# Grouped-query attention on one core: three reduced-precision value products instead of one full one, two units behind the scores, with normalisation on ScalarE and two steps on GpSimd

## Reference, cut to what matters

```python
nh, nkv, hd = 32, 8, 128
q = (x @ Wq).reshape(B, S, nh, hd).transpose(0, 2, 1, 3)
k = (x @ Wk).reshape(B, S, nkv, hd).transpose(0, 2, 1, 3)
v = (x @ Wv).reshape(B, S, nkv, hd).transpose(0, 2, 1, 3)
q = q * cos + rotate_half(q) * sin          # k likewise
logits = einsum('bhqd,bhkd->bhqk', q, repeat(k)) / sqrt(hd)   # causal mask
attn = softmax(logits)
out = einsum('bhqk,bhkd->bhqd', attn, repeat(v))
return out.transpose(0, 2, 1, 3).reshape(B, S, nh * hd) @ Wo
```

## Time and profile before

| | us |
|---|---|
| median of three runs | 2526.03 (2522.1 to 2527.65) |
| the profiled execution | 2533.18 |
| its span, first to last instruction | 2530.8 |
| the attention stage in it, from its first projection to its last merge | 1649.72 to about 2464 |
| one pass in it | 101.0 |

### The profile page before, as it was taken

One profiled execution on the slowest core, in us unless ns is written; L12 is line 12 of the kernel. 1 busy time (PEld: TensorE's weight loads), 2 busy tenths in 40 slices (PEclk: granted clock), 3 DMA queues, 4 the chain that ended last, 5 costly groups with the idle time before them and its releaser, 6 DMA issues. The chain is left out here.

```text
span 2530.8 us, 40532 instructions
## 1 busy us (share of the span) xinstructions
PE 2471.5 (98%) x12630; PEld 1861.0 (74%) x12630; DVE 1555.9 (61%) x2790; ACT 1392.1 (55%) x2155; POOL 1134.9 (45%) x1140
## 2 busy tenths in 40 slices
PE   8999999999999999999998999899999999999997
PEld 4677777777777777777775688778888888888874
DVE  6666666666666666666664522375756657557556
ACT  3677777777777777777776432232423424324231
POOL 1556555555555565556554243243434334334210
PEclk8999999999999999999999999999999999999998
DMA  6122222222222222222221422111001010010001
GB/s 213 42 45 55 45 53 47 51 53 44 53 46 57 46 53 44 53 46 54 45 53 38 139 88 88 65 44 42 17 25 41 0 41 17 25 41 17 1 3 52
DMA packets 47611, 125.38 MB, mean 50 GB/s; under 512 B 6034, under 2 KB 23442, under 8 KB 41427
## 3 DMA queue, kind: packets, MB, share of 16 engines
q1 hardware_dynamic: 47570, 124.85, 18.5%
HBM read 80.27 MB, written 10.49 MB: 36 GB/s over the span
## 5 line engine op out<-in xcount | busy, mean ns | idle before, releaser
L427 DVE TENSOR_REDUCE row_max<-ps_max 128x1 f32<-128x512 f32 x1024 | 670.4, 687 | 196.7 <-PE ps_max L517 174.9
L292 POOL TENSOR_TENSOR p_parts<-probs,p_parts 128x1024 f16<-128x1024 f32 x256 | 547.6, 2148 | 369.0 <-ACT p_parts L346 368.1
L341 ACT ACTIVATE probs<-ps_score 128x1024 f32<-128x1024 f32 x512 | 523.1, 1022 | 240.4 <-PE ps_score L533 218.6
L531 PE MATMUL ps_score<-Q,K 128*128 128x512 f32 x1024 | 408.1, 398 | 2.1 <-ACT probs L341 2.1
L533 PE MATMUL ps_score<-Q,K 97*128 97x512 f32 x1024 | 406.7, 397 | 0.0
L517 PE MATMUL ps_max<-KX,Q 68*128 68x512 f32 x1024 | 378.8, 411 | 2.2 <-DVE row_max L427 2.1
L421 DVE TENSOR_TENSOR Q<-ps_x,Q 64x512 fp32r<-64x512 f32 x254 | 175.1, 689 | 242.5 <-ACT Q L336 238.8
L346 ACT ACTIVATE p_parts<-probs 128x1024 f16<-128x1024 f32 x256 | 269.4, 1053 | 4.0
L517 PEld LDWEIGHTS ps_max<-KX,Q 68*128 68x128 f32 x1024 | 189.6, 190 | 75.0 <-issue 28.1
L531 PEld LDWEIGHTS ps_score<-Q,K 128*128 128x128 f32 x1024 | 194.2, 190 | 61.7 <-ACT probs L341 13.5
L533 PEld LDWEIGHTS ps_score<-Q,K 97*128 97x128 f32 x1024 | 195.0, 190 | 39.4
(11 more groups left out here) (269 smaller groups left out, 4387.6 us busy)
## 6 DMA issues: line engine op xcount, KB each, us to landing
Q<-Q SPq DMA_DIRECT2D x64, 512.0 KB, 4.3
ffn_raw<-in_w_ffn SPq DMA_DIRECT2D x22, 768.0 KB, 4.4
w_raw<-in_w_qrope SPq DMA_DIRECT2D x32, 512.0 KB, 3.6
wq_raw<-in_wq SPq DMA_DIRECT2D x8, 1024.0 KB, 5.5
wo_raw<-in_wo SPq DMA_DIRECT2D x8, 1024.0 KB, 4.8
content_k<-probs SPq DMA_DIRECT2D x8, 512.0 KB, 6.4
Q<-content_q SPq DMA_DIRECT2D x64, 64.0 KB
K<-content_k SPq DMA_DIRECT2D x64, 64.0 KB
```

The source lines that it names most:

```text
L292: pool.tensor_tensor(p_lo[:, j, :, :], probs[:, j, 0:PAIRED, :], p_hi[:, j, :, :], ALU.subtract)\
L341: act.activation(probs[:, j, 2 * half:2 * half + 2, :], ps_score[half][:, :, :], ACT.Exp, scale=SCALE).then_inc(exped, 1)
L427: dve.tensor_reduce(row_max[:, t, j:j + 1], ps_max[t % 2][:, :], axis=AXX, op=ALU.max)\
L531: pe.matmul(ps_score[half][:, k, :], K1[:, b, t * P:(t + 1) * P], Q1[:, b, j, :], start=True, stop=False)
```

## The change

1. The value product is made of three fp32r products per tile in place of one in float32. V and the turned probabilities therefore get a high and a low part: ACT writes the high ones, DVE the low ones (`low_values`, `low_turned`), out of the same PSUM bank.
2. On PE, `outputs(u-2)` and the third turn piece of u-2 stand in iteration u, the outputs behind the projection; turn pieces 0 and 1 of u-1 come last in the iteration. Turn piece k waits for the low part of the piece two before it (`t_low`), which frees its bank. The outputs of unit 6 stand behind the loop, and merges are ordered by head, so that those that need units 6 and 7 wait last (`o_low`). Turn piece 2 of unit 7 stands between two merges.
3. The four scalings of the probabilities are moved from DVE to ACT (L1493 becomes four activations with a scale); DVE keeps the reciprocal. `probs` is packed tightly.
4. The rope's sum is moved from DVE to POOL, in front of POOL's two steps.
5. ACT copies the output from PSUM to `o_raw`, and POOL makes its high and low part (`split_out`), in place of ACT and DVE.

```diff
--- before.py
+++ after.py
...
+        V = [buf(f"v_{k}", [P, NB, ST, P], F32R) for k in ("hi", "lo")]
+        by_sin = buf("by_sin", [P, 2, S])
         roped = buf("roped", [P, 2, S])
-        probs = buf("probs1", [P, 2, ST, S])
-        probsT = buf("probsT", [P, 3, S])
+        ROWS = [P * t * (t + 1) // 2 for t in range(ST + 1)]
+        probs = buf("probs1", [P, 2, ROWS[ST]])
+        TURNED = [(0, S), (S, S), (2 * S, 2 * P)]
+        probsT = [buf(f"probsT_{k}", [P, 2 * S + 2 * P], F32R) for k in ("hi", "lo")]
+        values_T = probs[:, 1, 0:NB * S].rearrange("p (b s) -> p b s", b=NB)
+        o_raw = buf("o_raw", [P, 2, S])
         O = [buf(f"o_{k}", [P, NB, GQ, S], F32R) for k in ("hi", "lo")]
         minus_max = buf("minus_max", [P, ST])
         sums = buf("sums", [P, 2, ST])
...
-
+            def rope(n, at, parts, take):
+
+                pool.wait_ge(taken, take + 1)
+                pool.sem_inc(gate_pool, 1)
+                pool.tensor_tensor(roped[:, at, :], roped[:, at, :], by_sin[:, at, :], ALU.add).then_inc(summed, 1)
                 pool.wait_ge(summed, n + 1)
                 pool.sem_inc(gate_pool, 1)
                 pool.tensor_copy(parts[0], roped[:, at, :]).then_inc(r_high, 1)
                 pool.wait_ge(r_high, n + 1)
+                pool.sem_inc(gate_pool, 1)
                 pool.tensor_tensor(parts[1], roped[:, at, :], parts[0], ALU.subtract).then_inc(r_low, 1)
 
...
+
+                pool.wait_ge(o_taken, ONE + i + 1)
+                pool.sem_inc(gate_pool, 1)
+                pool.tensor_copy(O[0][:, u % 2, u // 2, :], o_raw[:, u % 2, :]).then_inc(o_step, 1)
+                pool.wait_ge(o_step, i + 1)
+                pool.sem_inc(gate_pool, 1)
+                pool.tensor_tensor(O[1][:, u % 2, u // 2, :], o_raw[:, u % 2, :], O[0][:, u % 2, u // 2, :],
+                                   ALU.subtract).then_inc(o_low, 1)
+
+            pool.sem_inc(o_low, TWO)
             for b in range(NB):
...
-                    rope_query(r + u - 2, u, u % 2)
+                    rope_query(r + u - 2, u, u % 2, tk + take_query(u))
+                    if u >= 4:
+                        split_out(i + u - 4, u - 4)
                     if u == 2:
                         pool.wait_ge(wo_in, 16 * (kv + 1))
...
-                        rope_query(r + NU - 1 + 2 * b, b, 1)
+                        rope_key(r + NU - 2 + 2 * b, b, tk + take_next(2 * b))
+                        if b == 1:
+                            split_out(i + NU - 3, NU - 3)
+                            split_out(i + NU - 2, NU - 2)
+                        rope_query(r + NU - 1 + 2 * b, b, 1, tk + take_next(2 * b + 1))
                         if b == 0:
+                            split_out(i + NU - 4, NU - 4)
                             split_kv(1, s + n + 1)
+                    split_out(i + NU - 1, NU - 1)
                     for h in range(1, GQ):
                         split_q(h, s + n + 1 + h)
+                else:
+                    for u in range(NU - 4, NU):
...
+                act.wait_ge(inverted, i + 1)
+                for t in range(ST):
+                    row = probs[:, u % 2, ROWS[t]:ROWS[t + 1]]
+                    ins = act.activation(row, row, ACT.Copy, scale=inverse[:, t:t + 1])
+                ins.then_inc(normed, 1)
+
             def take_turned(kv, u, k):
...
 
             def take_outputs(kv, u):
 
                 i = NU * kv + u
                 act.wait_ge(pv_made, i + 1)
-                act.activation(O[0][:, u % 2, u // 2, :], ps_o[:, :], ACT.Copy).then_inc(o_high, 1)
+                act.wait_ge(o_low, i + 1)
+                act.activation(o_raw[:, u % 2, :], ps_o[:, :], ACT.Copy).then_inc(o_taken, 1)
 
...
-                softmax(i, 0)
+                ALL, BEGIN, REST = slice(0, ST), slice(0, 1), slice(1, ST)
+                softmax(i, 0, ALL)
+                normalise(i, 0)
                 values(kv, 0)
                 values(kv, 1)
                 turned_values(kv, 0)
                 turned_values(kv, 1)
                 for u in range(1, NU):
+                    if u >= 2:
+                        act.wait_ge(turned, 3 * (i + u - 1))
+                    softmax(i + u, u, BEGIN)
+                    if u >= 2:
+                        take_turned(kv, u - 2, 2)
+                    softmax(i + u, u, REST)
+                    if u >= 2:
+                        take_outputs(kv, u - 2)
                     take_turned(kv, u - 1, 0)
                     take_turned(kv, u - 1, 1)
-                    softmax(i + u, u)
-                    take_turned(kv, u - 1, 2)
-                    take_outputs(kv, u - 1)
+                    normalise(i + u, u)
+                take_turned(kv, NU - 2, 2)
+                take_outputs(kv, NU - 2)
                 for k in range(3):
                     take_turned(kv, NU - 1, k)
                 take_outputs(kv, NU - 1)
...
-                if not first:
-                    dve.wait_ge(summed, n)
                 if not first and not second:
...
-                dve.wait_ge(taken, take + 1)
-                dve.tensor_tensor(roped[:, at, :], roped[:, at, :], by_sin[:, :], ALU.add).then_inc(summed, 1)
 
...
+            def invert(i, u):
                 dve.wait_ge(exped, ONE + ST * (i + 1))
                 dve.reciprocal(inverse[:, :], sums[:, u % 2, :]).then_inc(inverted, 1)
-                dve.wait_ge(inverted, i + 1)
-                for t in range(ST):
-                    n = (t + 1) * P
-                    ins = dve.tensor_scalar(probs[:, u % 2, t, 0:n], probs[:, u % 2, t, 0:n], inverse[:, t:t + 1],
-                                            None, ALU.mult)
-                ins.then_inc(normed, 1)
-
-            def low_o(i, u):
-                dve.wait_ge(o_high, i + 1)
-                dve.tensor_tensor(O[1][:, u % 2, u // 2, :], ps_o[:, :], O[0][:, u % 2, u // 2, :], ALU.subtract)\
-                   .then_inc(o_low, 1)
-
-            dve.sem_inc(o_low, ONE)
+
+            def low_values(kv, b):
+                dve.wait_ge(v_high, NB * kv + b + 1)
+                dve.tensor_tensor(V[1][:, b, :, :], ps_t[b][:, :].rearrange("p (t n) -> p t n", t=ST), V[0][:, b, :, :],
+                                  ALU.subtract).then_inc(v_low, 1)
+
+            def low_turned(i, u, k):
+                dve.wait_ge(t_high, 3 * i + k + 1)
+                at, n = TURNED[k]
+                dve.tensor_tensor(probsT[1][:, at:at + n], ps_t[(u + k) % 2][:, 0:n], probsT[0][:, at:at + n],
+                                  ALU.subtract).then_inc(t_low, 1)
+
+            dve.sem_inc(t_low, TWO)
...
                 maxima(i)
-                normalise(i, 0)
+                invert(i, 0)
+                for b in range(NB):
+                    low_values(kv, b)
                 rope(r, ring + ring_query(2), (START + ring_query(2)) % 2, 0, tk, 0)
+
...
                     maxima(i + u)
-                    normalise(i + u, u)
+                    if u >= 2:
+                        low_turned(i + u - 2, u - 2, 2)
                     if u < NU - 2:
                         rope(r + u, ring + ring_query(u + 2), (START + ring_query(u + 2)) % 2, 0, tk + u, u % 2)
-                        low_o(i + u - 1, u - 1)
-                    else:
-                        for k in range(NU - u) if not last else ():
-                            at = 2 * (u % 2) + k
-                            rope(r + NU - 2 + at, ring + ring_next(at), (START + ring_next(at)) % 2, 1 - k, tk + take_next(at), k)
-                        low_o(i + u - 1, u - 1)
+                    elif not last:
+                        for at in (0, 1) if u == NU - 2 else (2,):
+                            rope_next(at)
+                    invert(i + u, u)
+                    low_turned(i + u - 1, u - 1, 0)
+                    low_turned(i + u - 1, u - 1, 1)
+                low_turned(i + NU - 2, NU - 2, 2)
                 if not last:
-                    rope(r + NU + 1, ring + ring_next(3), (START + ring_next(3)) % 2, 0, tk + take_next(3), 1)
+                    rope_next(3)
+                low_turned(i + NU - 1, NU - 1, 0)
+                low_turned(i + NU - 1, NU - 1, 1)
                 add_out(0)
-                add_out(1)
-                low_o(i + NU - 1, NU - 1)
-                for j in range(2, TT):
+                low_turned(i + NU - 1, NU - 1, 2)
+                for j in range(1, TT):
                     add_out(j)
 
...
                     pe.wait_ge(normed, i + 1)
-                if k == 2:
-                    pe.wait_ge(t_taken, 3 * i + 1)
+                pe.wait_ge(t_low, TWO + 3 * i + k - 1)
                 for tile, at in pieces[k]:
...
                 b = u % 2
-                pe.wait_ge(o_low, ONE + i)
-                for k, piece in enumerate(pieces):
-                    pe.wait_ge(t_taken, 3 * i + k + 1)
-                    for tile, at in piece:
```

(90 more changed lines are left out.)

31 lines of the change are left out of this document (17 added, 14 removed).

## The result

Over eight runs each, the changed kernel takes 2533.72 us (2530.87 to 2540.11) and the kernel before 2522.97 us (2518.66 to 2527.65). The ratio is 1.0043, with a 95% interval of 1.0028 to 1.0059: slower by 7 to 15 us, 10.8 by the medians. The forecast was +9 us. Of the runs behind the ratios of this document two stood far off and are left out: one of e2_query_before_turn, 2717 us at a granted clock of 0.845, and one of the kernel before, 4884 us.

What follows compares the result with a forecast made beforehand. PE, busy 98% of the span, was taken as the bound. Seven passes at +1.35 us (+9.4), some +1 before the first and -1 in the last gave some +9 us: 2535 us, range 2530 to 2545.

Steps and rivals of the forecast that it cites:

- The product: Outputs on PE: twelve fp32r products take 1.90 us against 1.97; a unit goes from 8.34 to 8.16 us.
- Scores(2): Start of a pass: PE waits 1.5 us for POOL's rope steps, as the rope stands behind V's low parts on DVE.
- Third piece of unit 6: End of a pass: PE waits 1.4 us for DVE's low part of the first turned piece.
- Value copy: Start of a pass, ACT: copy behind scalings of 1.45 us just hidden; at 2.1 it costs 0.4 us.
- Merge 0: End of a pass: head 3 on PE waits 0.25 us for unit 6's low output part.
- The pass: Each pass: waits of 1.5, 1.4 and 0.25 less 1.8 saved give +1.35 us; seven passes +9.4.
- Before the first pass: Ahead of the first scores: two ropes stand in series on POOL, some +1 us.
- The last pass: Last pass, without projections: new waits some 4 us against 3 before, and 2 us less work: -1.
- The cheaper product: Rival on PE's outputs: products cost under 1.90 us; at 1.72, 2523.5 us in all; chance 0.16.
- The absorbed waits: Rival at both ends of a pass: chains arrive in time, 2512 us, or 2523 with half absorbed; chance 0.2.
- GpSimd as the bound: Rival on POOL: rope's sum at 2.0 us, not 1.29, makes 8.2 us a unit; at least 2551; chance 0.09.
- The four equal part-products: Outputs on PE: three of four parts of 1.97 remain, 1.48 us; 2508 us in all; within the rival of chance 0.16.

Runs made afterwards that it cites:

- e2_query_before_turn: The changed kernel, with PE projecting the next pass's second query before the third turn piece of unit 6; 2529.99 us, ratio 1.0008 to the kernel before.
- e3: The changed kernel with rope of query 2 before V's low parts, and next pass's second query before unit 6's third turn piece; 2513.54 us, 0.9946.
- e4: The changed kernel with the rope's sum back on DVE; 2532.78 us, ratio 1.0037 to the kernel before.
- e8: e3 with the rope's sum back on DVE; 2518.16 us, ratio 0.9967 to the kernel before.
- e9: e3 with the four scalings of the probabilities back on DVE; 2572.86 us, ratio 1.0190 to the kernel before.
- e6: e3 with ACT copying the first projected values before the scaling of unit 0; 2507.66 us, ratio 0.9927 to the kernel before.
- e5: The changed kernel's order with the value product in plain float32, without low parts of V or turned probabilities; 2531.18 us, ratio 1.0017.

## Why the prediction was right, and where its sizes were off

- *Where the time is decided.* Right: PE was full before and waits of PE are the whole loss; with the two long ones gone, e3 is faster than the kernel before. That DVE's relief is worth nothing by itself holds for the sum in the changed kernel (e4). It doesn't hold once the two waits are gone (1 us a pass, e8), nor for the scalings: the prediction set no price on DVE and POOL slowing each other, and with POOL's new work the scalings in their old place on DVE cost 60 us (e9).
- *The product.* 1.90 was forecast for twelve products, 1.91 to 1.93 measured. The saving was undersized: the plain form costs 2.16 with what it leaves to its successor, and two transposes behind scores took 0.16 instead of 0.22. A unit is 8.09 us (1779.33 to 1787.41 is 8.08) against a forecast 8.16. That is some 4 us over the stage.
- *Scores(2).* The mechanism was right in each step: low parts of V in front, POOL's chain last, the exponentials close behind (e4). The wait was 1.74 us (1775.19 to 1776.93) and not 1.5. Of the difference, 0.18 is POOL's two gaps of 0.17 us where 0.08 was put; the late value copy moved both PE and the chain.
- *Third piece of unit 6.* 1.26 us against 1.4 forecast.
- *Value copy.* Forecast as just hidden, because I took 1.45 us for four scalings on ACT. They took 1.92, near my upper end, and the wait was 0.2 us, 0.34 with its aftermath (e6).
- *Merge 0.* 0.15 us, 0.25 forecast.
- *The pass.* 1.35 us longer forecast, 1.15 measured (102.16 against 101.01). *Before the first pass:* scores(0) waited 1.32 us for POOL, about 1 forecast. *The last pass:* -1 forecast; from its first projection to its last product it took 91.02 us against 90.89, so +0.1. By these rows the stage grew by 7 x 1.15 + 0.56 + 0.1 = 8.7 us, of which 0.56 lies ahead of the first pass, where PE also ran some products faster than before (granted clock 0.91 against 0.84). So the total came nearer than its parts: per pass the waits came to 3.5 us and not 3.15 (the value copy's included), the saving to 2.3 and not 1.8, and the seven passes were forecast 1.4 us too dear and the last 1.1 too cheap. That 8.7 stands so near to 9 is in part luck.
- *Rivals.* The cheaper product failed: it took no less than 1.90. The unit came out 0.07 us below the forecast, by the turns, and not 0.18. The absorbed waits and GpSimd as the bound both failed; POOL is 65 us of 102, as forecast (66). The four equal part-products that would fall to three have no support: 1.92 of 2.16 is not three quarters.

## What to carry to other kernels

When one engine is full, price a reorder by the places where its queue gets shorter in front of a wait: here work was moved to later in the pass, and at the pass's two seams the same chains, 2 to 4 us long, had nothing left to hide behind. Look at the seams of the loop first, where the steady state's order is broken; both losses were there, and two moved lines gave back 24 us. Before work is moved between VectorE and GpSimd, look for a place in the old trace where the two overlap on SBUF, and read the durations there; a mean, or the commonest row, hides it.

## What the runs showed of the hardware

- Scalings of 128 x 128 to 128 x 512 float32 on VectorE, SBUF to SBUF, took 1.27 us for four alone and 2.67 to 3.59 us with GpSimd work on SBUF beside them, whether that was a conversion, a subtraction or a sum; GpSimd's conversion went from 0.61 to 0.78 us. VectorE's subtraction from PSUM kept its 1.27 us for two beside GpSimd's subtraction (1810.49 in e9). The Trainium skill ("GPSIMD Engine Reference", Specifications) lists contention of GpSimd with VectorE instructions in a 2-port mode or with two SBUF inputs; the traces agree for the first kind, if the scalings run in that mode, which no row here names. They agree for the second: in e8 DVE's sum of two SBUF operands took 0.82 us and not 0.69 beside POOL's work, and POOL's subtraction 1.51 and not 1.29.
- A plain float32 product costs what follows it some 0.2 us. Transposes start 2.16 us after the outputs (e5). Scores start 1.97 us after them, but then take 2.49 us, where behind fp32r products they take 2.29. Transposes cost the scores behind them 0.09 (2.38).
- Four scalings of 1280 columns in all take 1.92 us on ScalarE, with the scale read from a tensor, where plain copies at the pace of 0.49 for 512 columns would give 1.3 (an estimate from the earlier trace rows: two copies take 1.09, one 0.60).
